# Pads and expert weights reordered on SP's queue in a gated cross-attention and mixture-of-experts layer

## What is computed

```python
logits = xf @ w_router                      # 4096 tokens, 8 experts
probs = softmax(logits); topk_w, topk_idx = top_k(probs, 2)
weights = sum(topk_w[..., None] * one_hot(topk_idx, 8), axis=1)
h = gelu(einsum('te,ieh->tih', xf, w1) + b1)    # 256 -> 1024
out = einsum('tih,ihe->tie', h, w2) + b2        # 1024 -> 256
out = sum(out * weights[..., None], axis=1)
x = x + tanh(g_ffn) * out
```

## Time and profile before

| | us |
|---|---|
| median of 3 runs (925.23 to 927.44) | 927.31 |
| the profiled execution | 927.44 |
| its span in the profile | 925.5 |
| TensorE busy in the span | 857.1 (93%) |
| VectorE busy | 645.4 (70%) |
| ScalarE busy | 514.2 (56%) |
| GpSimd busy | 332.1 (36%) |

### The profile page before, as it was taken

How to read it: one execution, slowest core, us unless ns; L and a number is a source line. 1 busy time by engine, 2 the same in 40 slices (tenths; PEclk the granted TensorE clock), 3 DMA queues, 4 the chain that set the end, 5 groups by cost and what they waited for, 6 DMA issues and landing times.

```text
span 925.5 us, 19447 instructions
## 1 busy us (share of the span) xinstructions
PE 857.1 (93%) x5968; PEld 657.7 (71%) x5968; DVE 645.4 (70%) x1500; ACT 514.2 (56%) x1371; POOL 332.1 (36%) x241
## 2 busy tenths in 40 slices
PE   3898899999999999998989999899999999999995
PEld 3654445544455454554449999899999999999995
DVE  6767766677766767667786778675765776575685
ACT  2668775787766877558742645243433443353462
POOL 2333223332376323662153227532232223232233
PEclk9999999999999999999999999899999999999998
DMA  4801000120012201120034449352343526352272
GB/s 125 242 1 49 1 1 1 46 94 1 2 58 80 92 1 46 58 92 1 1 109 116 114 105 268 82 138 45 74 107 47 136 37 150 46 140 47 34 221 31
DMA packets 71899, 70.31 MB, mean 76 GB/s; under 512 B 18593, under 2 KB 66977, under 8 KB 71841
## 3 DMA queue, kind: packets, MB, share of 16 engines
q1 hardware_dynamic: 57696, 52.73, 19.2%
q0 software_dynamic: 13152, 16.86, 10.5%
q10 hardware_dynamic: 992, 0.00, 0.1%
HBM read 44.04 MB, written 26.31 MB: 76 GB/s over the span
## 4 chain that ended last, share of the span: by engine, by line
PE 55%; issue 14%; DVE 11%; POOL 10%; ACT 5%; DMA 3%; DVEq 0%; POOLq 0%; SPq 0%; ACTq 0%
PE psS L1664 22%; PE psF L1860 10%; PE psO L1860 10%; POOL rr L676 6%; PE psO L1797 4%; POOL routed L686 4%; PE psS L1781 3%; DVE p_sum L1134 3%; PE psF L1664 2%; DMA out<-V,token_i 2%; PE psF L1828 2%; ACT sq L823 1%; ACT p_ring L867 1%; DMA xr<-in_x 1%; DVE qkd L1108 1%
## 5 line engine op out<-in xcount | busy, mean ns | idle before, releaser
L884 ACT ACTIVATE V<-psS,b_col 128x256 f32<-128x256 f32 x280 | 117.1, 471 | 216.2 <-PE psS L1664 205.4
L694 POOL DMA_INDIRECT out<-V,token_i x70 | 120.4, 1720 | 271.8 <-DVE V L1325 246.4
L676 POOL TENSOR_TENSOR rr<-ssm,minus_half 128x4 f32<-128x4 f32 (+1 forms) x72 | 119.9, 1665 | 254.3 <-DVE ssm L1098 254.1
L867 ACT ACTIVATE p_ring<-psS,shift 128x1024 f32<-128x1024 f32 x128 | 136.5, 1112 | 71.9 <-PE psS L1781 71.6
L1797 PE MATMUL psO<-p_ring,V 128*64 128x512 f32 x576 | 148.5, 612 | 1.5 <-ACT o_sb L855 1.5
L1134 DVE TENSOR_TENSOR p_sum<-p_sum,p_ring 128x1024 f32<-128x1024 f32 (+1 forms) x112 | 136.0, 1215 | 0.6
L1860 PE MATMUL psF<-ln_hi,K 128*128 128x256 f32 x560 | 123.3, 284 | 0.2 <-DVE K L1304 0.2
L1781 PE MATMUL psS<-Q,K 64*128 64x512 f32 x864 | 120.2, 409 | 0.6 <-ACT p_ring L867 0.5
L1860 PE MATMUL psO<-ln_hi,K 128*128 128x256 f32 x560 | 120.2, 278 | 0.0
L1781 PEld LDWEIGHTS psS<-Q,K 64*128 64x128 f32 x864 | 75.9, 184 | 61.0 <-issue 42.7
L1304 DVE TENSOR_TENSOR K<-V,K 128x512 fp32r<-128x512 f32 x140 | 97.1, 694 | 4.8
(11 more groups left out here) (289 smaller groups left out, 1764.0 us busy)
## 6 DMA issues: line engine op xcount, KB each, us to landing
xr<-in_L_ffn_w SPq DMA_DIRECT2D x11, 1024.0 KB, 7.9
xn<-in_L_ffn_w SPq DMA_DIRECT2D x11, 1024.0 KB, 5.3
lnf<-routed SPq DMA_DIRECT2D x35, 258.0 KB
routed<-pad_rows SPq DMA_DIRECT2D x17, 258.0 KB, 9.5
xr<-in_x SPq DMA_DIRECT2D x8, 512.0 KB, 4.4
xb<-in_x SPq DMA_DIRECT2D x4, 1024.0 KB, 5.9
out<-xb SPq DMA_DIRECT2D x4, 1024.0 KB
b_raw<-in_L_ffn_b SPq DMA_DIRECT2D x11, 128.0 KB, 3.4
```

Source lines behind the costliest of these rows:

```text
L676: pool.tensor_tensor(rr[0:p, c % 2, n], ssm[0:p, c % 2, n], minus_half[0:p, n], ALU.pow).then_inc(rr_ready, 1)
L694: pool.indirect_dma_start(out_rows, bass.IndirectOffsetOnAxis(ap=token_i[:, m:m + 1], axis=0), y_out[:, m, :], None, bounds_check=NTOK - 1 ...
L867: act.activation(p_ring[0:p, u % RING, :], psS[u % 2][0:p].rearrange("p a n -> p (a n)"), ACT.Exp, bias=bias).then_inc(exp_done, 1)
L884: act.activation(g32[:, q % 2, (c % 2) * TM:(c % 2 + 1) * TM], psH[q][:, (c % 2) * TM:(c % 2 + 1) * TM], ACT.Gelu_apprx_tanh, bias=b1_col[ ...
```

## The change

It touches only the program order of SP. The load of expert 3's w1 is moved ahead of the pads. The eight pads are split in two halves: pads 0 to 3 come before the load of expert 3's w2, pads 4 to 7 behind the loads of the rows of tile 7 and of expert 3's b1. The load of the rows of tile 7 comes behind the w2 load, and that of tile 8 stands last. All waits and transfers stay the same.

```diff
                 load_rows(5, kept_row(5))
                 load_b1(2)
                 load_rows(6, kept_row(6))
+                load_w1(3)
                 sp.wait_ge(pads_known, 1)
-                for e in range(NE):
+                for e in range(NE // 2):
                     pad(e)
+                load_w2(3)
                 load_rows(7, kept_row(7))
-                load_w1(3)
-                load_w2(3)
+                load_b1(3)
+                for e in range(NE // 2, NE):
+                    pad(e)
                 load_rows(8, kept_row(8))
-                load_b1(3)
                 sp.wait_ge(scattered, B * (32 * T))
                 sp.wait_ge(pads_filled, 16 * NE)
                 sp.wait_ge(plan_ready, 4)
```

## The result

The changed kernel takes 937.85 us (median; 937.55 to 938.14), the kernel before 926.86 us in the same comparison. By these medians it is 11.0 us slower. The ratio over all executions of the comparison is 1.0126, 95% interval 1.011 to 1.0142. The forecast was 934.5 us. The direction, the place and the chain of waits came out as predicted; the price of the queue did not, nor did the strict order in it. A later comparison gave 1.0127 (1.0094 to 1.0159).

A forecast was written before the change was run, and what follows sets the result against it. The prediction took TensorE, full behind the touched stretch, as the bound, so tile 7's delay reaches the end nearly whole: 927.44 us profiled plus 7.1 gives 934.5 us, range 929 to 938.5.

The forecast's parts named there:

- the chain of waits: Tile 7's rows land late; then turning, meta copy and plan lead to tile 7's first layer, starting at L + 9.7.
- the price of the queue: All-engine time on SP's queue ahead of and with rows 7: w1 3.0, four pads 4.0, w2 3.0, rows 1.0; 11.0 us.
- the strict order: SP's transfers are served in order of issue, so b1(3) and pads 4 to 7 come after rows 7.
- the landing L: Time when tile 7's rows arrive, on the before trace's clock: 581.9, within a range of 574.2 to 584.5.
- the margin of rows 9: Slack between rows 9's arrival and their turning on TensorE: falls from 3.0 to 1.2 us, at cost 0.
- the formula: End of tile 7's first layer at L + 15.7 against 590.53 before; a loss of 7.1 us.
- No gain from the early w1(3): SP's queue: w1(3) is issued only 0.3 us earlier, and its first reader comes beyond 600; no gain.
- the test: Check of the transfer prices on the kernel before, over 21 us of its trace: 22.2 summed against 22.1 measured.
- The Trainium skill's figure: About 358 GB/s of HBM per core would put L at 580.3 and the time at 932.9 us.
- No queueing: Rival at turn_tile(7): rows 7 served beside older transfers, L = 574.2, 926.8 us, not slower; chance 0.15.
- Late and cold: Rival: L = 584 and tile 7's first layer at the low clock, loss 11.1, 938.5 us; chance 0.1.
- Rows 9 too late: Rival at turn_tile(9): delayed pads 4 to 7 hold up scatters beyond the margin, loss 7.9, 935.3 us; chance 0.05.

The follow-up runs named there:

- The repeat: The changed kernel run again unaltered, for the scatter of the landing of tile 7's rows; ratio 1.0127 to the kernel before.
- experiments 2: The kernel before with only the split of the pads, pads 4 to 7 behind b1(3) and ahead of rows 8; ratio 0.9997.
- experiment 4: The changed kernel with pads 4 to 7 behind rows 8 instead of ahead of it; ratio 1.0141 to the kernel before.
- experiment 1: The changed kernel with rows 7 put back right behind w1(3), ahead of pads 0 to 3 and w2(3); ratio 1.0043 to the kernel before.
- experiment 11: The changed kernel with four dummy-row blocks at fixed addresses in place of pads 0 to 3, all real pads behind rows 8; ratio 1.0114.
- experiment 7: The changed kernel with GpSimd's add_rows(5) and all behind it waiting until tile 7's rows have landed; ratio 1.0114.
- experiment 10: The changed kernel with w1(3) behind rows 7, SP still waiting for w1_ready at the same place; ratio 1.0082 to the kernel before.
- experiments 6: The changed kernel with GpSimd's scatters 6 to 11 of the last sequence behind add_rows(6); rows 7 landed at tau 31.0, the kernel lost 20 us.

## Why the prediction was right in kind and short in size

*The chain.* Right, nearly term by term. From the landing L to the end of tile 7's first layer the sum had 15.7 us; the profile has 603.65 - 588.54 = 15.1. The plan started at L + 2.4 (forecast L + 2.5), the hole behind it was 0.98 us (about 1), tile 7's first layer took 5.99 us (6.0), the margin of rows 9 held in this profile. The loss by the formula with the measured L and the measured 15.1 is 32.3 + 15.1 - 36.4 = 11.0 us, which is the measured one. The profiles with the landings of the table bear the slope out: 5.4, 6.4, 5.8 and 10.8 us of lengthened tail for landings at 26.1, 27.3, 27.4 and 32.3, where the formula gives 4.8, 6.0, 6.1 and 11.0. The repeat lies above it, 13.5 us at 33.7 instead of 12.4; 0.39 us of that is the late rows 9.

*No gain from the early w1(3), none from the split, nothing from the late pads.* Right (experiments 2 and 4), but for one point that the prediction did not have: once rows 7 are on time, rows 8 behind the late pads are 1.49 us late (experiment 1).

*The landing.* This step failed: "In sum 16.0 at share 1.05 is 15.2 us", L = 581.9, tau 27.8. Measured were 32.3 (33.7 in the repeat), 4.5 us more. Start and share were right: the first traffic of w1 shows at 568.7, tau 12.4 (12.6 was put), and the mean share from there to the landing is 1.06. Too small was the work, and the view of DMA queues tells whose. The changed kernel, 568.7 to 588.5 (packets, MB, share; q1 is SP's queue, q0 GpSimd's):

```profile
q1 hardware_dynamic: 4379, 4.07, 80.9%
q0 software_dynamic: 720, 1.33, 24.7%
```

The shares times 19.8 us are 16.0 us of all engines for SP's queue, where the prediction had 11.0, and 4.9 us for GpSimd, where it had 5.0. Two things are in the 16.0. First the prices: in experiments 4 and 11, where SP's queue moved just the 3.55 MB ahead of and with rows 7, they took 14.4 and 15.6 us (shares of 0.780 and 0.797 in 18.4 and 19.6 us). Second the order: the prediction had b1 and pads 4 to 7 "served after rows 7", but here 0.5 MB of them were moved before the landing (0.2 MB up to 587.5, a microsecond before it: 3.78 MB). By these figures 3.4 to 4.6 of the 5.0 us are the price, and the rest is the order. What the order alone costs the landing is not settled: experiment 11, without such traffic, landed at 32.3 as well.

The landings of the table say the same of the prices. Four pads moved it by 6.2 to 7.6 us and were priced at 4.0 (3.8 at share 1.05); w2 with its bias moved it by 5.0 to 6.4 and w1 by 4.9, and each was priced at 3.0. These differences come from different orders and do not add up. GpSimd was priced right; yet holding most of it back brought only 1.7 us (experiment 7).

*Why the test did not catch it.* The prices were tested on a sum over 21 us of the kernel before, 22.2 against 22.1. In it SP's items are 14.0 and GpSimd's 8.2. By queue, the same stretch of before:

```profile
q1 hardware_dynamic: 4511, 4.18, 70.9%
q0 software_dynamic: 1003, 1.59, 33.6%
```

That is 14.9 us for SP and 7.1 for GpSimd. The test had too little for SP and, with four adds and eleven scatters (2.0 MB, where 1.59 MB were moved), too much for GpSimd. The two cancel there, and do not cancel in another order. The rows that could have told were single slices: from 566 to 569 the kernel before moved 173 GB/s at share 1.07, with the last pads under way:

```profile
566.00:569.00 3.00, 3.00 (x27) 3.00 (x26) 2.85 (x7) 2.86 (x4) 2.39 (x3) 1.00 1.07 173
```

The Trainium skill's figure (DMA: Bandwidth & Descriptors, Specifications, 358 GB/s as one core's share of HBM) gave, as an estimate, 932.9 us, which is further off. The trace does not agree with it as a rate of this stretch: the 18 us of full engines moved 287 GB/s, and the two microseconds shown in experiment 10 moved 414.

*The rivals.* No queueing is refuted: the unqueued landing would have been at 574.2, tau 20.1. Late and cold named nearly the right time, 938.5, by luck: it put the landing at 584 and it came at 586.4 on the clock of before, 2.4 us later, and it had tile 7's first layer cold, 1.9 us, where it was warm. Rows 9 too late did not happen in the profile of the changed kernel; in the repeat of it they were 0.39 us late and in experiment 4 0.71 us, so the margin of 1.2 us was not there in these.

*Open.* Why a pad costs about 0.8 us of all engines into an empty queue, 1.1 in the row of the start, and 2.0 behind w1 (0.264 MB / 150 GB/s x 1.12, experiment 7). Its address, its place, GpSimd's scatters and adds, b1 and b2 are out. That the queue ahead is full is not enough, since it was full at the start too. That transfers issued behind rows 7 are partly served before these have landed is shown by the bytes of the changed kernel and of experiment 10; what it costs rows 7 was not separated. Open too is where some 2 us of experiment 1 go.

## What to carry to other kernels

A small load that an engine waits for belongs ahead of the large transfers that nobody needs yet; here moving one load of 258 KB back on the queue took away 7 of 11 us. Price a queue from slices where one kind of transfer runs, under the load that it will meet, and split a test by queue, since several wrong terms can satisfy one sum. And follow a hole that you close to the next wait: the plan's 4.8 us gave nothing until the scatters behind it were moved as well.

## What the runs showed of the hardware

The DMA share stood above 1 while the rate fell to 150 to 176 GB/s in stretches of stores behind loads (experiments 6, 7 and 11, and 576 to 580 of the changed kernel), and stretches with loads of weights ran at 379 GB/s at a share of 1.04 (572 to 575 of the changed kernel) and 414 at 1.03 (experiment 10). A high share alone does not say that much is moved. On SP's queue 0.5 MB of what was issued behind rows 7 were moved before they landed, in the changed kernel and in experiment 10. TensorE stopped at 573.9 in the changed kernel and its granted clock was 0.50 (1.2 GHz) from the slice 579 on; it came back in the slice from 592, 4 us after work began at 588.5. In the kernel before, it fell 2.4 us after the stop at 577.8. A stop of 0.98 us left the clock up.
